# A last stage in another order: a list of steps per engine, six PSUM banks, and work moved from VectorE and GpSimd to ScalarE and TensorE

## What is computed

```python
# L2_ffn: 8 experts of rank 64, each token's top 2, weights from the input
h  = gelu(xr @ w1A[e].T @ w1B[e]);  ye = h @ w2A[e].T @ w2B[e]
out = out + mask * ye

# L3_attn: causal depthwise convolution with M = 21 taps, then two products
h_hatt = conv(x_c, w, padding=[(M - 1, 0)], feature_group_count=128)
return input_data @ W1 + h_hatt @ W2 + bias

# L3_ffn: blocks of 16 numbers rounded to fp4 (grid 0 .5 1 1.5 2 3 4 6) times a scale
scale = max(|xb|) / 6;  q = GRID[searchsorted(MID, |xb / scale|)] * sign(xb) * scale
gate = fp4(x) @ fp4(w_gate).T;  y = fp4(x) @ fp4(w_up).T     # 128 -> 352 wide
return fp4(silu(gate) * y) @ fp4(w_down).T
```

## Time and profile before

| | |
|---|---|
| median of 3 runs | 1663.84 us (1662.66 to 1664.72) |
| profiled execution | 1664.72 us, its span 1662.9 us |
| mean granted TensorE clock | 0.942 |
| TensorE busy | 1449.5 us, 87% |
| VectorE busy | 1337.0 us, 80% |
| ScalarE busy | 1032.7 us, 62% |
| GpSimd busy | 339.3 us, 20% |
| DMA | 64.13 MB, mean 39 GB/s |

### The profile page before, as it was taken

One profiled execution on the slowest core, in us unless ns is written; L12 is line 12 of the kernel. 1 busy time (PEld: TensorE's weight loads), 2 busy tenths in 40 slices (PEclk: granted clock), 3 DMA queues, 4 the chain that ended last, 5 costly groups with the idle time before them and its releaser, 6 DMA issues.

```text
span 1662.9 us, 22946 instructions
## 1 busy us (share of the span) xinstructions
PE 1449.5 (87%) x8235; PEld 658.6 (40%) x8235; DVE 1337.0 (80%) x2821; ACT 1032.7 (62%) x1903; POOL 339.3 (20%) x270
## 2 busy tenths in 40 slices
PE   6569999999768777899999999999999898794866
PEld 3432222222457465233333333333333345462645
DVE  7776777773567667888888999888888679998997
ACT  4457999998442212777777787777777665361322
POOL 4000000000113321111111111111111134455454
PEclk9889999999989889999999999999999988897877
DMA  3055556554100101000000000000000000000001
GB/s 90 21 116 135 148 146 151 147 145 142 48 1 1 66 1 64 1 1 1 1 1 1 1 14 14 1 1 1 1 1 1 26 1 1 0 1 0 7 13 32
DMA packets 44657, 64.13 MB, mean 39 GB/s; under 512 B 5376, under 2 KB 26112, under 8 KB 44160
## 3 DMA queue, kind: packets, MB, share of 16 engines
q1 hardware_dynamic: 44544, 62.67, 14.1%
HBM read 54.27 MB, written 7.34 MB: 37 GB/s over the span
## 4 chain that ended last, share of the span: by engine, by line
PE 55%; DVE 28%; issue 10%; ACT 4%; POOL 2%; DMA 0%; DVEq 0%; SPq 0%; POOLq 0%; ACTq 0%
PE ps L1957 11%; PE ps L1948 8%; PE ps L265 7%; PE ps L542 7%; PE ps L1927 4%; DVE p6ac L2499 4%; PE ps L1967 3%; DVE WA L2533 3%; PE ps L1937 2%; DVE xn L172 2%; PE ps L551 2%; PE ps L688 1%; DVE X L188 1%; DVE st L154 1%; POOL p4vn L2062 1%
## 5 line engine op out<-in xcount | busy, mean ns | idle before, releaser
L2044 ACT ACTIVATE p4E<-ps,p4mx,p4sc 128x512 f32<-128x512 f32 x512 | 392.6, 773 | 138.0 <-DVE p4mx L2003 138.0
L2001 DVE TENSOR_REDUCE p4mx<-ps 128x2 f32<-128x1024 f32 x256 | 312.5, 1221 | 63.0 <-PE ps L1948 60.8
L1957 PE MATMUL ps<-p4E,p4vn 128*64 128x512 f32 x1024 | 247.9, 604 | 9.2 <-POOL p4vn L2062 9.1
L1948 PE MATMUL ps<-p4T 64*128 64x512 f16 x1536 | 199.6, 379 | 3.9 <-ACT p4E L2044 3.2
L166 POOL TENSOR_TENSOR rs<-rs,cst 128x4 f32<-128x4 f32 x58 | 61.3, 1057 | 522.8 <-DVE rs L160 522.8
L2062 POOL TENSOR_TENSOR p4vn<-p4v,p4zs 128x512 f32<-128x512 f32 x64 | 66.7, 1042 | 496.2 <-DVE p4zs L2006 496.2
L265 PE MATMUL ps<-p1R,p1w1s 128*128 128x512 bf16 x512 | 144.8, 384 | 3.7 <-ACT xn L274 2.5
L274 ACT ACTIVATE p1g<-ps,WB 128x1024 f32<-128x1024 f32 x128 | 137.6, 1136 | 13.0 <-PE ps L265 12.3
L574 DVE SCALAR_TENSOR_TENSOR p1Pb<-ps,WB,p1sh 128x512 f32<-128x512 f32 x128 | 94.7, 748 | 57.8 <-PE ps L542 56.7
L542 PE MATMUL ps<-p1g,WB 128*32 128x512 f32 x512 | 136.3, 608 | 0.0
L542 PE MATMUL ps<-xn,WB 128*32 128x512 f32 x256 | 135.4, 612 | 0.3 <-DVE p1Pb L574 0.3
(11 more groups left out here) (359 smaller groups left out, 2699.5 us busy)
## 6 DMA issues: line engine op xcount, KB each, us to landing
p1sh<-gscr SPq DMA_DIRECT2D x128, 256.0 KB
p1R<-tscr SPq DMA_DIRECT2D x64, 128.0 KB, 5.2
tscr<-p1tp SPq DMA_DIRECT2D x24, 128.0 KB, 2.5
WA<-in_w SPq DMA_DIRECT2D x1, 2632.0 KB, 8.8
WB<-in_w SPq DMA_DIRECT2D x1, 2560.0 KB, 9.2
X<-in_x SPq DMA_DIRECT2D x8, 256.0 KB, 5.8
gscr<-p1gT SPq DMA_DIRECT2D x8, 256.0 KB, 5.4
out<-X SPq DMA_DIRECT2D x8, 256.0 KB, 2.3
```

What stands on the lines that cost most here:

```text
L1948: y = p.e.matmul(ps[:, at + hh, :], t[rows, q, 128 * j:128 * j + 128], t[rows, 2 + r, :], start=o == 0, stop=o == 2)
L1957: t = p.e.matmul(ps[64 * hh:64 * hh + 64, 7, :], vn[n % 2][:, j, 64 * hh:64 * hh + 64], E[2 * (n % 2) + hh][:, j, :], start=j == 0, stop=j ...
L2001: v.e.tensor_reduce(m, ps[:, at:at + 2, :], AX, ALU.max).then_inc(v.own.h, v.one())
L2044: a.e.activation(self.E[2 * i + hh][:, j, :], ps[:, at + hh, :], ACT.Exp, bias=self.mx[i][:, j, hh:hh + 1], scale=pre.sc[:, 1, 0:1], accum ...
```

## The change

What it does, all but the first item in the last stage:

- The low-rank weights are split in 4 pieces of 128 partitions, not 8 of 64; the two DMAs are gone. "up" is 3 products of 64-row halves, both experts of a pair side by side, in 4 steps with 2 Gelus each; "inner" is split by one ScalarE and one VectorE instruction.
- `order()` takes an engine's name and reads a string of letters written for this engine; each letter is the next step of its kind. There is no common sequence any more. The DVE string interleaves taps with the other chains one by one.
- Six banks (1, 4, 0, 2, 3, 5) serve all short results in turn.
- Convolution taps: no part on ScalarE and GpSimd. `PT` is 10, 2, 2, 5, 6, 10, 12, 11 taps on TensorE (sum 58, was 39), the rest on VectorE (102 with the first of each block, was 81).
- Layernorm rows: VectorE computes a shift of 4 columns, ScalarE scales and shifts the rows.
- Rounding constant: ScalarE squares the scaled tile to bf16 and adds a base, instead of mask, maximum and product on VectorE. The extra factor is inside the scaling. The weights' subtraction and last product stay on VectorE, those of x and h on GpSimd.
- Products: VectorE reads the up half from PSUM; ScalarE's copy is gone.

The diff, cut:

```diff
-        for hh, r in enumerate(halves):
-            sp.wait_ge(k.sem("uhi"), 4 * hh + 4)
-            sp.wait_ge(k.sem("ulo"), 4 * hh + 4)
-            sp.e.dma_start(self.up[halves[1 - hh], :, :, hh, :], self.up[r, :, :, hh, :]).then_inc(k.sem("up5").h, 16)
...
+    def ln_shift(self, v, chain, n, b):
+        r = slice(4 * b, 4 * b + 4)
+        v.wait_ge(self.sem(chain, "rstd"), n + 1)
+        v.e.scalar_tensor_tensor(self.sh[:, r], self.mv[:, r, 0], -1.0, self.rs[:, r], ALU.mult, ALU.mult).then_inc(self.sem(chain, "shift").h, 1)
+
+    def ln_scaled(self, a, chain, b, at):
+        for j in range(4):
+            i = 4 * b + j
+            a.e.activation(self.xn[:, at + j, :], self.X[:, i, :], ACT.Identity, bias=self.sh[:, i:i + 1], scale=self.rs[:, i:i + 1]).then_inc(self.sem(chain, "row").h, 1)
...
-        v.e.tensor_scalar(iv, sc, 1.0 + 2.0 ** -22, None, ALU.mult).then_inc(v.own.h, v.one())
+        v.e.reciprocal(iv, sc).then_inc(v.own.h, v.one())
...
-        v.e.tensor_tensor(y, y, self.bc(iv), ALU.mult).then_inc(v.own.h, v.one())
...
-        v.e.tensor_scalar(mag.bitcast(I32), x.bitcast(I32), 0x7F800000, None, ALU.bitwise_and).then_inc(v.own.h, v.one())
...
-        v.e.tensor_scalar(mag, mag, 1.0, MAGIC, ALU.max, ALU.mult).then_inc(v.own.h, v.one())
...
+        v.e.scalar_tensor_tensor(y, y, 1.0 - 2.0 ** -22, self.bc(iv), ALU.mult, ALU.mult).then_inc(scaled.h, 1)
+        yield
+
+    def square(self, a, sq, base, mag, n):
+        rows, cols = self.x.shape
+        sq = sq[0:rows, 0:cols]
+        a.wait_ge(mag, n)
+        a.e.activation(sq, self.x, ACT.Square, scale=self.ROOT).then_inc(a.own.h, a.one())
+        a.wait_ge(a.own, a.n)
+        a.e.activation(self.mag, sq, ACT.Identity, bias=base[0:rows, 0:1]).then_inc(mag.h, 1)
...
-    M, TP, GT = 21, 8, 5
-    PT = [4, 4, 4, 4, 4, 4, 7, 8]
-    AT = {1: 0, 2: 1, 3: 2, 4: 3, 5: 4, 6: 5, 7: 6, 9: 7}
+    M, TP = 21, 12
+    PT = [10, 2, 2, 5, 6, 10, 12, 11]
+    KINDS = {
+        "a": "gates", "b": "turn", "c": "inner", "d": "tap products", "e": "up", "f": "mix", "g": "down", "h": "turn w", "i": "turn x",
+        "j": "gate up", "k": "turn h", "l": "out rows", "m": "down7", "n": "stats", "o": ("quant w", 0), "p": ("quant w", 1),
+        "q": ("quant w", 2), "r": ("quant w", 3), "s": ("quant w", 4), "t": "rows", "u": ("quant w", 5), "v": ("quant w", 6),
+        "w": "tap", "x": "add taps", "y": "stats7", "z": "down out", "A": ("quant x", 0), "B": ("quant x", 1), "C": ("quant x", 2),
+        "D": ("quant x", 3), "E": ("quant x", 4), "F": ("quant x", 5), "G": "product", "H": ("quant h", 0), "I": ("quant h", 1),
+        "J": ("quant h", 2), "K": ("quant h", 3), "L": ("quant h", 4), "M": "out add", "N": "finish", "O": "square w", "P": "normal x",
+        "Q": "square x", "R": "square h", "S": "taps", "T": ("quant x", 6), "U": ("quant x", 7), "V": ("quant h", 5),
+        "W": ("quant h", 6),
+    }
+    ORDER = {
+        "tensor": (
+            "aabcddbecedeefegeceebdgheeeibdcfejgjjjeeedeidcejgfeeedkkblkkjmejgcjeeedefgcckkeeeikdkjjjmjebgfeeedekgkkkibmjjjj"
+            "ldifjjkkjjkkbdmdifjjjjkkkkdmdifjjjjkkkkmijjjjkkkkmkkkkm"),
...
+        "gpsimd": (
+            "SnnnnSnySTUSyTUSVWyVWnTUSVWyVWTUSVWyVWTUnVVWSWyTUVWVWyTUVWVWyTUVVWWVWVW"),
...
-        self.bank = {u: (1, 4, 0)[i % 3] for i, u in enumerate(uses)}
-        self.last = {u: uses[i - 3] for i, u in enumerate(uses) if i > 2}
+        uses = [u for what, x in self.order("tensor") for u in self.banks(what, x)]
+        self.bank = {u: (1, 4, 0, 2, 3, 5)[i % 6] for i, u in enumerate(uses)}
+        self.last = {u: uses[i - 6] for i, u in enumerate(uses) if i > 5}
...
+                for o, (q, r) in enumerate(Attention2.PARTS):
+                    for hh, rows in enumerate((slice(0, 64), slice(64, 128))):
+                        t = p.e.matmul(ps[:, bank[what, (x, hh)], :], low.up[rows, r, n % 4, 128 * f:128 * f + 128], self.aT[n % 4][rows, q, :],
+                                       start=o == 0, stop=o == 2)
...
-                    p.e.matmul(o, self.ag[i][:, 128 * j:128 * j + 128], w6("W2"), start=False, stop=False, skip_group_check=True)
...
+                v.e.tensor_tensor(self.hq[g % 4][:, 352 * j:352 * j + 352], ps[:, self.bank["gate up", (x, 1)], 0:352], self.sg[n % 4],
+                                  ALU.mult).then_inc(k.sem("h7").h, 1)
...
-                a.e.copy(self.hq[g % 4][:, 352 * j:352 * j + 352], ps[:, bank[what, (x, 1)], 0:352]).then_inc(k.sem("gu out").h, 1)
...
-                    t = g.e.tensor_tensor(ag[:, :], ag[:, :], self.at[n - 1][:, :], ALU.add)
```

More of the change, by code:

```diff
@@ L2074, in sync @@
         k = self.k
-        ahead = self.low.sync(sp)
         for what, x in self.order():
@@ L2081, in sync @@
                 k.load_w(sp, x)
-            elif what == "ahead":
-                step(ahead)
     def ended(self, line):
@@ new lines, in order, with banks @@
+    def order(self, engine):
+        left = {kind: iter(among) for kind, among in self.steps().items()}
+        for letter in self.ORDER[engine]:
+            kind = self.KINDS[letter]
+            yield kind[0] if isinstance(kind, tuple) else kind, next(left[kind])
+    def banks(self, what, x):
+        if what in ("gates", "down", "out rows", "turn", "turn x", "turn h", "down7"):
+            return [(what, x)]
+        if what == "inner":
+            return [("inner", x), ("spread", x)]
+        if what in ("up", "gate up"):
+            return [(what, (x, 0)), (what, (x, 1))]
+        if what == "turn w":
+            return [(what, c) for c in range(3)]
+        return []
@@ L2313, in released, with evacuated @@
     def released(self, p, use):
+        if use in self.last:
+            self.evacuated(p, self.last[use])
+    def evacuated(self, p, use):
         k = self.k
-        if use not in self.last:
-            return
-        what, x = self.last[use]
+        what, x = use
         if what == "gates":
@@ L2339, in tensor @@
         w, w6 = lambda n: k.Wt(5, n), lambda n: k.Wt(6, n)
-        for what, x in self.order():
+        for what, x in self.order("tensor"):
             if what == "gates":
@@ L2614, in gpsimd @@
         quants = {}
-        for what, x in self.order():
+        for what, x in self.order("gpsimd"):
             if what == "stats":
```

402 lines of the change are left out of this document (153 added, 249 removed), and 13 rows, old and new, of the table AGAIN.

## The result

The changed kernel takes 1582.12 us (median of four runs, 1581.32 to 1584.15); the kernel before took 1663.64 in the same comparison. The ratio is 0.9512, with a 95% interval of 0.9495 to 0.9528: 81.5 us less, where 55 less was forecast. The direction held; the measured time lies 1 us under the low end of the range, in rival (b)'s part.

What follows compares the result with a forecast made beforehand. VectorE's list of work was taken to bound the last stage: 202 us work, 44 waits for GpSimd and 36 gaps make 282, after 1326 us a span of 1608, so 1609 us; range 1583 to 1640.

Steps and rivals of the forecast that it cites:

- rival (b): Last stage: VectorE's waits for GpSimd mostly vanish in the new order, 12 us left; 1577 to 1592 us, chance 0.14.
- Work taken from VectorE: Last stage: VectorE's 301.7 us busy falls to 227.2 with the changes, 202 of it work without waits for GpSimd.
- The waits for GpSimd after it: Last stage, VectorE: 71 GpSimd operations stay at 0.64 us of wait each; 44 us taken, 17 to 66 possible.
- the Trainium skill's rule: VectorE instructions with two SBUF inputs and GpSimd instructions reading SBUF exclude each other; half of GpSimd's 111 us, 56 us.
- The products: L2533 on VectorE: reading the up half from PSUM makes 32 products 0.51 us each, 31.9 us off 48.2.
- Gaps: VectorE idle in the last stage: 4 us at the start, 20 in the middle, 12 in the tail, together 36.
- Against 282 it is the second bound, not the first: TensorE in the last stage: 250 to 262 us busy at the present clock, 212 to 223 at full clock.
- Rival (a): Last stage: TensorE and in-order queues set the pace, middle gaps 40 to 50 us; 1629 to 1639 us, chance 0.22.
- rival (c): ScalarE: Square isn't in the Gelu and Silu tables, so 35 table loads, not 12; 1624 us, chance 0.07.
- signs: Last stage: L2533's successor at 0.5 us, taps of two kinds, VectorE busy 240 to 250, 12 table loads, ScalarE near 170.
- sign of being wrong: VectorE gaps over 50 us released by TensorE or ScalarE, or mean tap time under 0.8.
- Rival (d): Last stage: TensorE drops to its lower clock and becomes the bound; at 0.65 1691 us, slower, chance 0.04.

Runs made afterwards that it cites:

- the short GpSimd operations: Changed kernel with GpSimd's subtraction and last multiplication of x and h cut to 16 columns (48 operations): 1575.05 us, ratio 0.9452.
- the three relief runs: Changed kernel with 16 of VectorE's taps cut to 8 columns, ratio 0.9522; with 16 of TensorE's taps left out, 0.9524; with both, 0.9484.

## Why the prediction was off by 27 us

The stage was put together as 202 + 44 + 36 = 282 us and came out as 199 + 27 + 29 = 255. So 17 of the 27 us are the waits, 7 the gaps and 3 the work. This is an account of VectorE's list; as TensorE is level with it, the 17 us needn't turn into time one for one (of the 22.4 us of excess that the short GpSimd operations removed, 8 to 10 came back).

**Work taken from VectorE: right.** 199 us undisturbed, for 202 forecast. The products are flat at 0.52, the shifts 0.16 instead of 0.2, the three-operand scaling costs what the two-operand one did (L2118 has a median of 692 ns for 512 columns, L2120 had 686).

**"The waits for GpSimd after it": the step that failed.** It spread 66.4 us evenly over 103 operations, found the share of two-operand work unchanged, and carried 0.64 us to each of the 71 operations that stay, 44 us. Half of the 66.4 were the products' 31.9, which it had just taken off as gone. Measured are 26.6, 0.37 each. The share of work with two SBUF operands was the wrong quantity, since GpSimd's operations don't come at random moments: an in-order queue behind semaphores puts them beside the same neighbours each time. The trace of before shows this when each long VectorE instruction is paired with the GpSimd operation that overlaps it most. Of its 78.0 us of excess, 29.5 lie beside the additions L2629, 22.4 of it on taps and rows (the run without the additions has 28.6 and the same 22.4), and 32.7 are products beside L2153 and L2157; some 16 are everything else. These two pairs were being dissolved, so 16 plus what the new order would make was the sum to write. What it would make, some 10 us (taps 9.6), the trace of before doesn't show. Rival (b), with 0.14, put the waits at 12 us, and its times, 1577 to 1592, take in the measured one; the prediction's objection to it, that nothing in GpSimd's list waits for such a moment, missed that the order itself fixes the neighbours. The estimate that the prediction made from the Trainium skill's rule, half a GpSimd operation each or 56 us, is farther off still: it too took the moments as random.

**The products: right sum, half of the cause.** 31.9 us off came true, but in the new order 24 of them go without the PSUM operand and only 9 depend on it: the changed kernel with SBUF products shows 10 long ones of 32, the old order with the same instructions 29. What the operand alone would have done in the old order is open.

**Gaps: 29 us for 36.** The start kept 0.4 us, where 4 were left; the middle to 1567 has 16.5, where 20 stood; the tail 12.4, where 12 stood. The six banks, costed at little because TensorE wasn't the bound, are worth 12 us here for two of the three added. TensorE is as near the bound as VectorE in the changed kernel, which would explain it; that this is the cause is argued, not shown.

**"Against 282 it is the second bound, not the first": not in a stage of 255.** TensorE is busy 231.6 us, between the 212 to 223 of full clock and the 250 at the old clock. It is 91% busy and ties with VectorE, as the three relief runs show. Rival (a), that TensorE and in-order queues set the pace at 302 to 312, had its mechanism half right: TensorE does beside VectorE, at 255.

**Other steps.** 12 table loads at 1.28 us, as counted, so Square is in both tables and rival (c) is out; the idle time before them is 0.3 and 0.1 us for six each. ScalarE is busy 170.4 for 172, GpSimd's list has 71, attention 2 gave nothing that can be told. Of what the prediction named as signs, only VectorE's busy time, 225.5 for 240 to 250, missed, and neither sign of being wrong came: they didn't test the size of the waits apart. Rival (d) needed a clock under 0.71; the stage has 0.96. Still, its number wasn't idle: the moved work in the old order ran at 0.75 and 6% slower.

**What the size of the gain goes by.** The list of moved operations doesn't make it: they lose 103 us in the old sequence (1.0618) and win 81 in the new (0.9512). With the same SBUF products, the order for each engine with six banks is the difference between 1.0618 and 0.9582, 172 us. The prediction priced the order only as a doubling of small gaps. The old list of operations in the new order and banks wasn't run, so what the order gives without the moved work is open, and so is the part of the banks beyond the 12 us between four and six.

## What to carry to other kernels

Group the waits between two engines by pairs of lines before scaling them: a change that dissolves a pair takes its whole wait along, and a change of order can take most of it without touching the instructions. Moving work to an idle engine whose queue is in order puts a wait for everything ahead of it into the chain, so move the work and its place in that queue together. When two engines are level, relieving one can show nothing; relieve both in one run before calling either harmless.
